# Attention of a four-layer block: values held still in narrow column tiles, probabilities streamed, softmax sums from tiles of ones, output bias by a product

## What is computed

```python
q, k, v = heads(x @ Wq + bq), heads(ctx @ Wk + bk), heads(ctx @ Wv + bv)   # 16 heads of 16
scores = q k^T / 4                       # layer 0 adds a bias per head, layer 3 masks
p = softmax(scores, axis=-1)             # over 64 context rows
out = concat_heads(p @ v) @ Wo + bo      # layer 0 has no bq, bk, bv, bo
x = x + tanh(g) * out                    # layer 0 has a gelu block in between
```

## Time and profile before

| what | value |
|---|---|
| median of 3 runs | 1632.23 us (1629.98 to 1634.14) |
| the profiled execution | 1628.77 us, its span 1627.0 us |
| PE busy over the span | 1381.6 us (85%) |
| DVE busy | 1222.4 us (75%) |
| ACT busy | 768.9 us (47%) |
| POOL busy | 369.0 us (23%) |
| products with the values (L1135) | 1024 instructions, 138.3 us busy |
| reciprocals of the sums (L1002) | 64, 16.1 us busy |

### The profile page before, as it was taken

How to read it: one execution, slowest core, us unless ns; L and a number is a source line. 1 busy time by engine, 2 the same in 40 slices (tenths; PEclk the granted TensorE clock), 3 DMA queues, 4 the chain that set the end, 5 groups by cost and what they waited for, 6 DMA issues and landing times.

```text
span 1627.0 us, 25891 instructions
## 1 busy us (share of the span) xinstructions
PE 1381.6 (85%) x9890; PEld 1263.5 (78%) x9890; DVE 1222.4 (75%) x2366; ACT 768.9 (47%) x1314; POOL 369.0 (23%) x294
## 2 busy tenths in 40 slices
PE   4897997797997399999389569968998999999995
PEld 4786885576895389999388458957886889999994
DVE  5796778788696679877389768976876848888773
ACT  4445441112455167776355324225455216676672
POOL 2241001012000137764101430000000013454442
PEclk9998998799898589999699888989998999999997
DMA  4332100010002178886300000000002026777783
GB/s 140 93 103 93 40 19 1 1 36 28 1 1 110 64 233 231 241 229 177 122 1 1 7 0 1 1 10 1 2 1 105 1 91 216 240 203 223 218 244 114
DMA packets 45438, 148.23 MB, mean 91 GB/s; under 512 B 11651, under 2 KB 22582, under 8 KB 35574
## 3 DMA queue, kind: packets, MB, share of 16 engines
q1 hardware_dynamic: 30038, 124.93, 22.3%
q0 software_dynamic: 15296, 21.90, 7.3%
HBM read 126.03 MB, written 22.87 MB: 92 GB/s over the span
## 4 chain that ended last, share of the span: by engine, by line
PE 59%; DVE 24%; ACT 7%; issue 4%; DMA 3%; POOL 1%; POOLq 1%; SPq 1%; ACTq 0%; DVEq 0%
PE PS L307 40%; PE PS L1135 6%; PE PS L1096 3%; PE PS L1119 3%; DVE X L2182 2%; PE PS L1370 1%; DVE RA L297 1%; ACT Y L225 1%; PE PS L1128 1%; POOLq L2904 1%; PE PS L1112 1%; PE PS L1776 1%; DVE RA L1754 1%; ACT RA L482 1%; DMA FA<-in_Wo 1%
## 5 line engine op out<-in xcount | busy, mean ns | idle before, releaser
L307 PE MATMUL PS<-RA 128*128 128x256 f32 (+3 forms) x6204 | 935.1, 310 | 83.4 <-DVE RA L297 18.4
L307 PEld LDWEIGHTS PS<-RA 128*128 128x128 f32 x6204 | 852.5, 196 | 139.0 <-issue 52.4
L1681 POOL DMA_INDIRECT sum_rows<-Y,KT x78 | 151.4, 1941 | 196.9 <-ACT Y L1722 166.4
L271 POOL TENSOR_TENSOR rstd<-vareps,neghalf 128x4 f32<-128x4 f32 x36 | 36.8, 1023 | 535.8 <-DVE vareps L248 216.8
L1135 PE MATMUL PS<-VBF,FA 128*128 128x136 f32 x1024 | 138.3, 290 | 4.0 <-ACT FA L897 3.9
L1670 POOL DMA_INDIRECT Y<-normed_rows,KT x78 | 88.2, 1130 | 217.6 <-DVE KT L1463 157.0
L1135 PEld LDWEIGHTS PS<-VBF,FA 128*128 128x128 f32 x1024 | 127.4, 196 | 9.5 <-ACT FA L897 6.2
L897 ACT ACTIVATE FA<-PS 128x1024 f32<-128x1024 f32 x64 | 65.6, 1025 | 105.3 <-PE PS L1096 105.3
L1754 DVE TENSOR_TENSOR RA<-FA,RA 128x2048 fp32r<-128x2048 f32 x46 | 105.3, 2288 | 10.9 <-ACT RA L1714 10.7
L1700 ACT ACTIVATE FA<-PS,unit_bias 128x256 f32<-128x256 f32 (+1 forms) x184 | 71.4, 443 | 80.0 <-PE PS L307 68.7
L1823 DVE TENSOR_TENSOR RA<-FA,RA 128x1024 fp32r<-128x1024 f32 (+1 forms) x46 | 80.9, 1759 | 24.7 <-ACT RA L1747 24.7
(11 more groups left out here) (315 smaller groups left out, 1893.9 us busy)
## 6 DMA issues: line engine op xcount, KB each, us to landing
FA<-in_eup SPq DMA_DIRECT2D x46, 1024.0 KB, 7.3
FA<-in_edown SPq DMA_DIRECT2D x23, 1024.0 KB, 6.7
FA<-in_edown SPq DMA_DIRECT2D x23, 512.0 KB, 3.8
FA<-in_fside SPq DMA_DIRECT2D x16, 512.0 KB, 3.5
sum_rows<-X SPq DMA_DIRECT2D x2, 2048.0 KB, 7.4
normed_rows<-Y SPq DMA_DIRECT2D x2, 2048.0 KB, 10.3
FA<-fp_rows SPq DMA_DIRECT2D x1, 2112.0 KB, 12.1
X<-in_x SPq DMA_DIRECT2D x4, 512.0 KB, 8.8
```

Source lines behind the costliest of these rows:

```text
L307: ins = pe.matmul(dst, stat(a, k), mov(b, k), start=(first and n == 0), stop=(last and n == len(todo) - 1))
L1681: pool.indirect_dma_start(out=sum_rows, in_=rows_out[p][:, t, :], in_offset=None, compute_op=ALU.add, out_offset=bass.IndirectOffsetOnAxis ...
```

## The change

In the product with the values the operands change places. The values of a pair of heads (`VB`, now 32 columns: 16 of one head on the upper 64 context rows, 16 of the other on the lower) are stationary, and `pt` streams with 128 columns. The four pairs of one half of the features go to four column tiles of 32, which write partitions 0 to 31, 32 to 63 and so on of bank 6: features by tokens, already turned. A second set of the same shape with `head_ones` as stationary operand writes each head's sum, once for each of its 16 features, into the other half of the bank. That is 16 calls per tile where there were 8, and a call is still two instructions. The two transposes (L1128) go.

DVE takes the reciprocal of the whole 128 x 256 region of sums into `rinv` (L1015 of the changed kernel) and multiplies (L1016). ACT and DVE make `ot` from `osb` instead of PSUM, and wait for the former reader (`y_ready`) in place of the transposes.

The output bias is no longer added on DVE. One more product per tile (L1150) starts the accumulation of the output projection: `sel_r` (ones on rows 0 and 32) times `bo_r` (the bias rounded on row 0, what the rounding left on row 32). To make them, POOL sets three memsets at the start of layers 1 to 3, ACT makes two copies after the last queries, and DVE one subtraction on 32 partitions, ahead of its loop. Filling `VB` takes 4 ACT instructions per layer instead of 8, and POOL's 16 memsets of ones become 2.

```diff
-VC = P + HC
+VW = 2 * DK
...
-            rsum = small[:, 32:32 + H]
+            rinv = fview(8960, D)
...
                     if slot.has(-1):
-                        slot.wait(act, ot_ready, -1, 1)
-                        act.activation(ot[:, 0], PS[:, 7, 0:D].rearrange("p (k t) -> p k t", k=KC), ACT.Copy).then_inc(ot_hi, 1)
+                        slot.wait(act, o_norm, -1, 1)
+                        slot.wait(act, y_ready, -1, 0)
+                        act.activation(ot[:, 0], osb[:, p, :].rearrange("p (k t) -> p k t", k=KC), ACT.Copy).then_inc(ot_hi, 1)
...
-                    dve.wait_ge(bo_in, 16 * l)
+                    low = slice(LOW_ROW, 2 * LOW_ROW)
+                    dve.wait_ge(wo_hi, 2 * l + 1)
+                    dve.tensor_tensor(bo_r[low], bo_row[low], bo_r[low].bitcast(F32), ALU.subtract).then_inc(wo_ready, 1)
...
-                        o = PS[:, 6, 0:KC * VC].rearrange("p (k v) -> p k v", k=KC)
-                        steps(dve.reciprocal(rsum.rearrange("p (k h) -> p k h", k=KC), o[:, :, P:VC]))
...
+                        steps(dve.reciprocal(rinv, PS[:, 6, D:2 * D]))
+                        dve.tensor_tensor(osb[:, p, :], PS[:, 6, 0:D], rinv, ALU.mult).then_inc(o_norm, 1)
...
-                            steps(dve.tensor_tensor(tmp, y, bo_row, ALU.add))
                             x = X[:, bass.ds(t, 1), :]
-                            dve.scalar_tensor_tensor(x, tmp.unsqueeze(1), gates[:, l:l + 1], x, ALU.mult, ALU.add).then_inc(fin_done, 1)
+                            dve.scalar_tensor_tensor(x, y.unsqueeze(1), gates[:, l:l + 1], x, ALU.mult, ALU.add).then_inc(fin_done, 1)
...
                         slot.wait(pe, pt_sb, 0, 1)
+                        slot.wait(pe, o_norm, 0, 0)
                         for k in range(KC):
-                            for c in range(4):
-                                ins = pe.matmul(PS[:, 6, k * VC:(k + 1) * VC], pt[:, 4 * (c // 2) + 2 * k + c % 2, :],
-                                                VB[:, t // HT, 4 * k + c, :], start=(c == 0), stop=(c == 3))
+                            for at, weights in ((k * P, VB[:, t // HT, 4 * k:4 * k + 4, :]),
+                                                (D + k * P, head_ones.unsqueeze(1).to_broadcast([P, 4, VW]))):
+                                for c in range(4):
+                                    ins = pe.matmul(PS[c * VW:(c + 1) * VW, 6, at:at + P], weights[:, c, :],
+                                                    pt[:, 4 * (c // 2) + 2 * k + c % 2, :], start=True, stop=True)
                         ins.then_inc(o_ready, 1)
...
+                        if not first:
+                            pe.matmul(PS[:, 7, D:2 * D], sel_r, bo_r, start=True, stop=False)
```

More of the change, by code:

```diff
@@ L371, in gpsimd @@
                                 allow_small_or_imprecise_dtypes=True))
[L372 to L375, removed]
+                for half in range(2):
+                    steps(pool.memset(head_ones[half * S2:(half + 1) * S2, half * DK:(half + 1) * DK], 1.0))
                 self.all_consts = steps.n
@@ L491, in scalar_keys @@
                         vd = VD[rows, self.l, b, :].rearrange("p (c t d) -> p t c d", t=2, d=DK)[:, half]
[L492 to L495, removed]
+                        ins = act.activation(VB[rows, b, :, half * DK:(half + 1) * DK], vd, ACT.Copy)
                 ins.then_inc(self.keys_ready, 1)
@@ L892, in scalar @@
                     queries_hi(3)
+                    act.wait_ge(kv.consts, kv.all_consts + 3 * l)
+                    act.activation(sel_r, sel_raw, ACT.Copy)
+                    act.wait_ge(bo_in, 16 * l)
+                    act.activation(bo_r, bo_row, ACT.Copy).then_inc(wo_hi, 1)
                 def work(slot, steps):
@@ L1035, in work @@
                     if slot.has(-1):
+                        t, p = slot.tile(-1)
                         slot.wait(dve, ot_hi, -1, 1)
-                        dve.tensor_tensor(ot[:, 1], PS[:, 7, 0:D].rearrange("p (k t) -> p k t", k=KC), ot[:, 0].bitcast(F32),
+                        dve.tensor_tensor(ot[:, 1], osb[:, p, :].rearrange("p (k t) -> p k t", k=KC), ot[:, 0].bitcast(F32),
                                           ALU.subtract).then_inc(ot_split, 1)
@@ L1122, in work @@
                         ins.then_inc(s_ready, 1)
-                    if slot.has(-1):
-                        t, p = slot.tile(-1)
-                        slot.wait(pe, o_norm, -1, 1)
-                        slot.wait(pe, fin_done, -1, 0)
-                        for k in range(KC):
-                            ins = pe.transpose(PS[:, 7, k * P:(k + 1) * P], osb[:, p, k * P:(k + 1) * P], ident[:, :])
-                        ins.then_inc(ot_ready, 1)
                     if slot.has(0):
@@ L1139, in work @@
                         slot.wait(pe, ot_split, -1, 1)
+                        slot.wait(pe, fin_done, -1, 0)
                         if slot.first + slot.p == 1:
-                            pe.wait_ge(wo_ready, l + 1)
+                            pe.wait_ge(wo_ready, 2 * l + 1)
+                        if not first:
+                            pe.matmul(PS[:, 7, D:2 * D], sel_r, bo_r, start=True, stop=False)
                         split_matmuls(pe, PS[:, 7, D:2 * D], range(KC), lambda a, k: ot[:, a, k, :],
-                                      lambda m, k: wo[:, m, k, :]).then_inc(y_ready, 1)
+                                      lambda m, k: wo[:, m, k, :], first=first).then_inc(y_ready, 1)
                 for t in range(FIRST_SLOT, LAST_SLOT + 1):
```

28 lines of the change are left out of this document (18 added, 10 removed).

## The result

The changed kernel takes 1675.0 us (median of 4 runs, 1673.09 to 1676.63) against 1631.41 us for the kernel before, measured beside it: a ratio of 1.0269, 95% interval 1.0256 to 1.0282. It is slower, by 43.6 us; the forecast was 1678. The profiled span is 1673.5 us against 1627.0.

The account below looks back on a forecast made before the run. PE set the pace of plain slots, DVE only 0.2 us faster in layer 1. Loops 46.3, gating -1.3, ahead of loops +1: 46 us on 1628.8 gives 1674.8, plus 3.5 for the runs' median: 1678 us; range 1666 to 1704.

Parts of the forecast that it names:

- DVE's price for a wide reciprocal: Reciprocal of 256 elements a partition in the attention loops: 1753 ns at 6.25 ns an element, 1.50 us more per tile.
- The rival of an instruction a third dearer an element: DVE's wide reciprocal takes 2.3 us, 32 us more in all, 1710 us; chance 0.03.
- The break-even: Reciprocal price on DVE from about 1.0 us downward at which the faster rival decides, 46 us over some 60 slots.
- that rival: Wide reciprocal on DVE costs 0.42 us like others of its width; PE sets the pace, 1604 to 1627; chance 0.05.
- The loops: Four attention loops: DVE's added work less its free time leaves 14.2, 12.95, 14.15 and 4.95 us, sum 46.3.
- The waits at a loop's end: DVE's free time lost at each loop's end, where it has little left to do: 1.4 us for every layer.
- DVE's busy time: Net addition on DVE per tile: 1.50 us in layer 0, 1.05 in layers 1 to 3; 22.5 and 15.75 a loop.
- The product with the values: PE's product in column tiles: 16 steps of 0.109, 1.74 us; bounds half that step, or 32 steps.
- The gating with a source in PSUM: Layer 2's gating beside POOL returns from 1.78 to 0.49 us: -1.3 us, bounds -3 and +2.
- TensorE's clock: Rival: longer DVE slots lower PE's clock; single drops cost little, a loop at half clock +150 us or more; chance 0.03.
- New waits: Product and ACT's copy into `ot` wait for DVE's normalisation: no cost while DVE sets the pace.
- ahead of the loops: In layers 1 to 3 one more DVE instruction moves the next start by 0.33 us: 1.0 us in all.

Follow-up runs that it names:

- the half-width run: Changed kernel with the reciprocal of only the first 128 of 256 columns, used for both halves: 1623.13 us, ratio 0.9938 to the kernel before.
- the copy at 0.41 us: Changed kernel with the wide reciprocal replaced by a copy of the same region, division left out: 1596.83 us, ratio 0.9794 to the kernel before.
- the doubling: Changed kernel with the 32 instructions of the product of values and sums issued twice a tile: 1677.54 us, ratio 1.0280 to the kernel before.
- the bias product alone: Kernel before with only the output bias moved from DVE's addition to a PE product, without column tiles: 1631.76 us, ratio 1.0005.
- three orders: Changed kernel, reciprocal as exp(-ln(sum)) on ACT: behind next exponentials 1626.56 us; ahead of them 1650.96; behind them, DVE's multiplication and gating after next subtraction, 1592.70.

## Why the prediction was right, point by point

- **DVE's price for a wide reciprocal** was the term that decided, and it was 1742 ns against the 1753 that the slope of the earlier trace rows gave. The rival of an instruction a third dearer an element falls: at 943 ns for 128 and 1742 for 256 the slope stays 6.24 ns.
- **The break-even.** "It decides from about 1.0 us a reciprocal downward": the half-width run puts it at 1.07 us, and the copy at 0.41 us gave 1596.8, below the 1604 to 1627 of that rival.
- **The loops.** Forecast +14.2, +12.95, +12.85 (with the gating's gain) and +4.95, together 45; measured +16.7, +13.3, +12.2 and +3.2, together 45.4. That the sum is better than its parts is luck: two errors cancel. A loop grows by as much as DVE's busy time grows, less what its idle time shrinks, and the rows of the loops before and after give both. DVE was left idle for 6.2, 4.3, 3.5 and 3.8 us, 17.7 in all and not "about 12"; the forecast took 2.9 in each loop, 1.5 of gaps and 1.4 of waits at its end. So it was short by 3.3, 1.4, 0.6 and 0.9. DVE's busy time grew by 21.7, 14.75, 13.25 and 13.1, where the forecast had 22.5, 15.75, 14.45 (less the gating's 1.3) and 15.75: too much by 0.8, 1.0, 1.2 and 2.6. Taken together that is +2.5, +0.4, -0.6 and -1.7, the errors of the four loops.
- **The waits at a loop's end** ("so 1.4 are lost") were mis-sized. The last two tiles' waits of DVE in layer 0, which answer to the earlier trace rows:

```profile
152.12 0.43 DVE L1047 TENSOR_TENSOR RA<-FA,RA 128x256 fp32r<-128x256 f32 x1 [0.58 <-ACT RA L912]
153.84 1.76 DVE L1015 RECIPROCAL FA<-PS 128x256 f32<-128x256 f32 x1 [0.88 <-PE PS L1141]
158.45 0.43 DVE L1047 TENSOR_TENSOR RA<-FA,RA 128x256 fp32r<-128x256 f32 x1 [2.07 <-ACT RA L912]
```

  They make 3.53 us, 2.1 over the 1.4, which is most of the 2.5 that layer 0 lies above its forecast. In layers 1 to 3 the same waits make 3.06, 2.11 and 2.48.
- **DVE's busy time** was taken to grow by the full price of what is added. The price per tile was right: the slot that was 4.61 (456.36 in the earlier trace rows) became 5.64 (478.74 above), both with the small instruction of every fourth tile (L217, now L218), so +1.03 against +1.05. The durations of DVE's rows in the four loops, added up, grew by 22.9, 16.3, 14.5 and 16.1 us. But an instruction that follows another at once lies over its last 80 ns or so, and one that comes after a wait does not: 1.3, 1.4, 1.2 and 2.9 us of the growth went into that overlap. Layer 3 has most of it: in the kernel before, 25 instructions of its loop came after a wait, in the changed one 2.
- **The product with the values** was mis-sized, by a factor of two: taken as 16 steps of 0.109 = 1.74 us. What the doubling adds is 0.88 us, eight steps of 0.110. The starts in the trace show why: the instructions start in fours, within 20 ns of each other in the first four (6 to 7 ns apart) and within 50 in the later ones, where the first is some 30 ns ahead, and each four comes 0.109 us after the last. Since instructions on one narrow tile stand 0.109 apart, four at a time means that all four tiles run together, not two passes of one beside one of the next. The range had that value as its lower bound, "16 steps of half of 0.109, which changes nothing", and it changes nothing here; it would matter once DVE is out of the way, which no run here shows. (The Trainium skill's TensorEngine Tiling (Array Packing), Key Properties, on different tiles loading and multiplying in parallel: the trace now agrees for column tiles too.)
- **The gating with a source in PSUM** was right for the mechanism, which two other runs show better than the changed kernel. POOL and DVE in order of time in layer 2, first with the bias product alone, then with the copy in place of the reciprocal:

```profile
897.54 2.40 POOL L691 TENSOR_TENSOR VD<-Y,VD 128x1024 f32<-128x1024 f32 x1 [3.40 <-DVE Y L683]
898.00 0.47 DVE L1033 SCALAR_TENSOR_TENSOR X<-PS,gates,X 128x256 f32<-128x256 f32 x1
...
879.70 2.36 POOL L687 TENSOR_TENSOR VD<-Y,VD 128x1024 f32<-128x1024 f32 x1
880.63 1.71 DVE L1047 TENSOR_TENSOR RA<-FA,RA 128x256 fp32r<-128x256 f32 x1
```

  The gating from PSUM, in the midst of POOL's instruction, takes its usual 0.47 us, where it was 1.78 from SBUF. What the prediction set against it came true there too: the low half of the turned output, now with both sources in SBUF, is held and takes 1.71 instead of 0.41. In the changed kernel itself neither was put to the test: the gating (0.47 at 936.77) started 0.4 us before POOL's instruction ended, the low half (0.41 at 939.55) 0.1 before. With the bias back on DVE and the gating reading SBUF again, it took no more than 0.49 us, since POOL had just ended. So the gain of 1.3 us came at least in part from the shifted times. The kernel before had two such gatings in that loop (1.35 and 1.78 us), of which the forecast priced one; that is part of the 1.2 us of layer 2.
- **TensorE's clock** fell to 0.85 to 0.97 of the full level over the loops, where the forecast had spoken of single drops, with PE waiting 1.4 to 1.9 us for DVE in many slots. "Single drops cost little, since PE has slack" holds for the plain slots. It fails in the last slot of a loop, where PE has no slack and ran at half clock (0.50, 0.50 and 0.53 in layers 1 to 3): at least 3.7 us by the doubled product. That cost is in the waits at a loop's end, which the forecast took at 1.4 us as in the kernel before, where those slots ran at the full clock.
- **New waits** at nothing: in plain slots no row of DVE has a wait. And **ahead of the loops** at +1.0: outside the four loops the span grew by 46.5 - 45.4 = 1.1 us. What the single parts there took was not separated, the loops' ends behind the last reciprocal, "taken as 0", among them.
- **The range.** Its ends don't follow from their words: all free time but the gaps (35.1 - 6 = 29.1 us) less the layer 2 gain gives 1632.3 + 69.75 + 1 - 29.1 - 1.3 = 1672.6, not 1666, and none of it 1703, not 1704. The measured 1675.0 lies between either pair. (Layer 2's slot of 6.08 us should be 6.10 by its own terms.)

## What to carry to other kernels

Price an instruction by its width from the trace before building on it, here the reciprocal at 6.25 ns an element, and ask of every gain which engine sets the pace after the change: the bias on PE was worth 0 us in sum in one kernel and 13 in the other. When work moves to an engine with free time, its place in that engine's in-order queue decides, and with it the order on the engine that waits for it: follow the loop of waits once around a tile and add it up, as the same two instructions gave 1627, 1651 and 1593 us in three orders.

## What the runs showed of the hardware that was not expected

- Matmuls on four column tiles of 32 with 128 streamed columns start within 50 ns of each other, and eight waves of four take 0.88 us more: 0.028 us for an instruction that alone takes 0.109 to the next.
- A logarithm and an exponential of 128x256 on ACT take 0.37 and 0.42 us, together less than half of the 1.74 us of DVE's reciprocal of the same shape.
- PE with twice the product was granted 0.98 to 1.00 of the full clock and ended three loops 0.5 to 1.6 us sooner than PE with half of it: more work in an engine's waits shortened the stretch behind them.
